# Latent attention: spreading transfers of full height, mean squares and denominators in one slot and one PSUM bank, division before the last additions

## The reference, cut to what matters

```
xn = layernorm(x, ln_x_g, ln_x_b)
ln = layernorm(latents, ln_l_g, ln_l_b)
q = (ln @ Wq).reshape(b, m, h, d).transpose(0, 2, 1, 3)
kv = jnp.concatenate([xn @ Wkv, ln @ Wkv], axis=1)
qn = rmsnorm(q, qn_g) * scale
kn = rmsnorm(k, kn_g)
sim = jnp.einsum('bhid,bhjd->bhij', qn, kn)
attn = jax.nn.softmax(sim.astype(jnp.float32), axis=-1).astype(sim.dtype)
out = jnp.einsum('bhij,bhjd->bhid', attn, v)
return out @ Wout + bout
```

## Time and profile before

| | |
|---|---|
| median of 3 runs | 1456.08 us |
| profiled execution, its own time | 1462.04 us |
| its span | 1460.3 us |
| TensorE busy (matmuls) | 1300.3 us, 89% |
| VectorE, ACT, GpSimd busy | 811.0, 637.5, 558.7 us |
| granted TensorE clock, mean of the span | 0.949 |
| spreading transfers of roots, of denominators | 232 and 124, 64.0 KB each |

### The profile page before, as it was taken

One profiled execution on the slowest core, in us unless ns is written; L12 is line 12 of the kernel. 1 busy time (PEld: TensorE's weight loads), 2 busy tenths in 40 slices (PEclk: granted clock), 3 DMA queues, 4 the chain that ended last, 5 costly groups with the idle time before them and its releaser, 6 DMA issues. The chain is left out here.

```text
span 1460.3 us, 20536 instructions
## 1 busy us (share of the span) xinstructions
PE 1300.3 (89%) x7179; PEld 561.9 (38%) x7179; DVE 811.0 (56%) x1364; ACT 637.5 (44%) x1187; POOL 558.7 (38%) x517
## 2 busy tenths in 40 slices
PE   5879789759997899999999999999967998887998
PEld 2214332238972333333333333333234774223443
DVE  4767677363336566655665666566455444623654
ACT  4454535442225555545553555454332444453222
POOL 1012201057421646554665555556605770310000
PEclk9999899779999999999999999999977999797999
DMA  9500400249622022222222222222051124000530
GB/s 267 215 1 12 117 6 1 100 170 370 245 104 65 12 45 46 44 44 41 47 44 44 44 44 45 43 45 44 22 188 35 52 52 127 1 1 0 118 72 15
DMA packets 68593, 109.14 MB, mean 75 GB/s; under 512 B 13278, under 2 KB 51550, under 8 KB 67742
## 3 DMA queue, kind: packets, MB, share of 16 engines
q1 hardware_dynamic: 56524, 93.80, 24.0%
q0 software_dynamic: 4544, 9.32, 2.3%
q10 hardware_dynamic: 7424, 4.72, 1.1%
HBM read 76.56 MB, written 11.04 MB: 60 GB/s over the span
## 5 line engine op out<-in xcount | busy, mean ns | idle before, releaser
L2693 ACT ACTIVATE a_prob<-a_TP 128x512 f32<-128x512 f32 x256 | 139.0, 595 | 161.6 <-PE a_TP L2448 161.6
L2844 DVE TENSOR_REDUCE a_lat<-a_SP 128x2 f32<-128x1024 f32 x128 | 156.1, 1220 | 85.0 <-PE a_SP L2412 85.0
L2980 POOL TENSOR_TENSOR a_acc<-a_prob 128x512 f32<-128x512 f32 x64 | 80.0, 1270 | 219.4 <-PE a_MS L2472 216.9
L2444 PE MATMUL a_TP<-a_qn,a_kn 64*128 64x512 f32 x512 | 146.7, 641 | 1.5 <-ACT a_prob L2693 1.5
L2460 PE MATMUL a_MS<-a_prob,a_V 128*64 128x512 f32 x512 | 129.5, 605 | 0.2 <-ACT a_prob L2693 0.2
L3543 DVE TENSOR_REDUCE a_nm<-a_A 128x8 bf16<-128x616 f32 x84 | 66.8, 795 | 39.2 <-PE a_A L3226 39.2
L2984 POOL TENSOR_TENSOR a_acc<-a_acc,a_prob 77x512 f32<-77x512 f32 x64 | 79.8, 1268 | 0.0
L2989 POOL TENSOR_TENSOR a_acc<-a_acc,a_prob 128x512 f32<-128x512 f32 x64 | 79.8, 1268 | 0.0
L2866 DVE TENSOR_TENSOR a_acc<-a_acc,a_prob 128x512 f32<-128x512 f32 x64 | 75.6, 1221 | 6.4 <-ACT a_prob L2693 6.3
L3757 POOL TENSOR_TENSOR a_on<-a_osb,a_rden 128x512 f32<-128x512 f32 x9 | 11.5, 1281 | 163.8 <-ACT a_osb L3426 163.8
L2444 PEld LDWEIGHTS a_TP<-a_qn,a_kn 64*128 64x128 f32 x512 | 39.7, 184 | 80.0 <-issue 51.3
(11 more groups left out here) (565 smaller groups left out, 2738.2 us busy)
## 6 DMA issues: line engine op xcount, KB each, us to landing
ring_w<-in_F_w SPq DMA_DIRECT2D x64, 512.0 KB, 12.3
a_rn<-a_rms_rows SPq DMA_DIRECT2D x232, 64.0 KB, 2.4
a_rden<-a_den_rows SPq DMA_DIRECT2D x124, 64.0 KB, 2.1
f_wide<-weight_rows SPq DMA_DIRECT2D x24, 256.0 KB, 5.5
a_maskT<-in_maskT SPq DMA_DIRECT2D x1, 2304.0 KB
a_biasT<-in_biasT SPq DMA_DIRECT2D x1, 2304.0 KB
f_b<-in_F_b SPq DMA_DIRECT2D x1, 2048.0 KB, 7.9
token_rows<-f_xtok ACTq DMA_DIRECT2D x8, 256.0 KB, 5.8
```

Of the source, the lines that this page charges most:

```text
L2444: nc.tensor.matmul(TP[0:n, h, :], keys(h), qn[half(h), r % 4, :], start=True, stop=False)
L2693: nc.scalar.activation(prob[0:n, 2 * k + h, :], TP[0:n, h, :], ACT.Exp, bias=rowneg[0:n, b:b + 1] if k == 0 else 0.0).then_inc(p_ready, 1)
L2844: nc.vector.tensor_reduce(lat[:, g % 2, 2 * u:2 * u + 2], SP[:, :, :], AX.X, ALU.max, negate=True).then_inc(s_used, 1)
L2980: nc.gpsimd.tensor_tensor(acc[:, h, :], prob[:, 2 + h, :], prob[:, 4 + h, :], ALU.add).then_inc(added, 1)
```

## The change

It has four parts.
- **Transfers.** Each root transfer now takes 32 source rows and writes all 128 partitions of `rn` (two for q, two for k, where there were four and four); each denominator transfer takes 64 rows and writes all 128 partitions of `rden` (two for four). The denominators' tiles change places for that. SP's order in a round is q, k, denominators as before in rounds up to 7, and q, denominators, k from round 8 on. A round issues six transfers of 128 KB where it issued twelve of 64 KB.
- **Statistics.** The denominators go to columns 256 to 511 of the bank, the mean squares stay in 0 to 255. `means(r + 3)` moves from step 1 to step 2, directly ahead of `sums(r - 1)`; `values(r - 1, 4)` moves from step 2 to step 1. TensorE no longer waits for the clip between them. Instead VectorE's clip waits for the denominators' matmuls (`den_made`), and ACT's logarithm of the denominators for the clip (`ms_clipped`).
- **Order behind it.** On VectorE `keep_output` stands ahead of reduction 3 and the clip behind it. On ACT `rms` moves behind the third exponentials, directly ahead of `denominators`.
- **Division.** On GpSimd `divide(r - 1)` moves ahead of the third pair of additions.

```diff
--- before.py
+++ after.py
@@ -2270,28 +2270,33 @@
                 sp.dma_start(blk[:, :], d["blk64"]).then_inc(blk_in, 16)
                 sp.dma_start(Wv[:, :], d["A2_Wv"]).then_inc(v_in, 16)
                 sp.dma_start(Wo[:, :, :], d["A2_Wo"]).then_inc(o_in, 16)
+                def spread_roots(g, j, normed, spread):
+                    sp.wait_ge(ms_rms, g + 1)
+                    sp.wait_ge(normed, g)
+                    for n in range(2):
+                        at = 32 * (2 * j + n)
+                        sp.dma_start(rn[:, j, n * HS:(n + 1) * HS],
+                                     rms_rows[at:at + 32, :].rearrange("i (c t) -> i c t", c=1)
+                                     .broadcast_to([32, 4, HS])).then_inc(spread, 16)
+
+                def spread_denominators(r):
+                    sp.wait_ge(den_ready, r + 1)
+                    if r:
+                        sp.wait_ge(o_normed, r)
+                    for n in range(2):
+                        sp.dma_start(rden[:, n * HS:(n + 1) * HS],
+                                     den_rows[HD * n:HD * n + HD, :].rearrange("i (c t) -> i c t", c=1)
+                                     .broadcast_to([HD, 2, HS])).then_inc(den_spread, 16)
+
                 for r in range(R):
-                    g = r + RAW
-                    if g < R:
-                        sp.wait_ge(ms_rms, g + 1)
-                        for j, normed, spread in ((0, q_normed, q_spread), (1, k_normed, k_spread)):
-                            sp.wait_ge(normed, g)
-                            for n in range(2):
-                                for h in range(2):
-                                    at = 32 * (2 * j + n) + 16 * h
-                                    sp.dma_start(rn[half(h), j, n * HS:(n + 1) * HS],
-                                                 rms_rows[at:at + 16, :].rearrange("i (c t) -> i c t", c=1)
-                                                 .broadcast_to([16, 4, HS])).then_inc(spread, 16)
-                    if r:
-                        sp.wait_ge(den_ready, r)
-                        if r >= 2:
-                            sp.wait_ge(o_normed, r - 1)
-                        for h in range(2):
-                            for n in range(2):
-                                at = 32 * (2 * h + n)
-                                sp.dma_start(rden[half(h), n * HS:(n + 1) * HS],
-                                             den_rows[at:at + 32, :].rearrange("i (c t) -> i c t", c=1)
-                                             .broadcast_to([32, 2, HS])).then_inc(den_spread, 16)
+                    if r + RAW < R:
+                        spread_roots(r + RAW, 0, q_normed, q_spread)
+                    if r >= 2 * B:
+                        spread_denominators(r - 1)
+                    if r + RAW < R:
+                        spread_roots(r + RAW, 1, k_normed, k_spread)
+                    if 0 < r < 2 * B:
+                        spread_denominators(r - 1)
 
             @block.tensor
             def _(pe):
@@ -2468,8 +2473,8 @@
                             mm = nc.tensor.matmul(DEN[half(h), :], ones64[:, :], acc[:, h, :], start=True, stop=True)
                             continue
                         for n in range(2):
-                            at = 32 * (2 * h + n)
-                            mm = nc.tensor.matmul(DEN[at:at + 32, 0:HS], ones64[:, 0:32],
+                            at = 32 * (2 * n + h)
+                            mm = nc.tensor.matmul(DEN[at:at + 32, HS:S], ones64[:, 0:32],
                                                   acc[:, h, n * HS:(n + 1) * HS], start=True, stop=True)
                     mm.then_inc(den_made, 1)
 
@@ -2553,16 +2558,14 @@
                             project(r + 3)
                         if s == 1 and r:
                             values(r - 1, 3)
-                        if s == (1 if r else 2):
+                            values(r - 1, 4)
+                        if s == 2:
                             if r == 0:
                                 pe.wait_ge(n_shifted, B + 1)
                             if r + 3 < R:
                                 means(r + 3)
-                        if s == 2 and r:
-                            values(r - 1, 4)
-                            if r + 3 < R:
-                                pe.wait_ge(ms_clipped, r + 4)
-                            sums(r - 1)
+                            if r:
+                                sums(r - 1)
                         if s == 3:
                             if p == 0 and b:
                                 output(b - 1, O, range(NP))
@@ -2700,11 +2703,13 @@
 
                 def denominators(r):
                     act.wait_ge(den_made, r + 1)
+                    if r + 4 < R:
+                        act.wait_ge(ms_clipped, r + 5)
                     if r < R - 1:
-                        nc.scalar.activation(lnd[:, 0:HS], DEN[:, 0:HS], ACT.Ln).then_inc(den_log, 1)
+                        nc.scalar.activation(lnd[:, 0:HS], DEN[:, HS:S], ACT.Ln).then_inc(den_log, 1)
                         act.wait_ge(den_log, r + 1)
                         if r:
-                            act.wait_ge(den_spread, 64 * r)
+                            act.wait_ge(den_spread, 32 * r)
                         nc.scalar.activation(den_rows[:, :], lnd[:, 0:HS], ACT.Exp, scale=-1.0).then_inc(den_ready, 1)
                         return
                     nc.scalar.activation(lnd[:, :], DEN[:, :], ACT.Ln).then_inc(den_log, 1)
@@ -2754,7 +2759,7 @@
                         if k == (0 if r else 1) and r + 3 < R:
                             square_q(r + 3)
                             square_k(r + 3)
-                        if k == (1 if r else 3) and r + 3 < R:
+                        if k == (2 if r else 3) and r + 3 < R:
                             rms(r + 3)
                         if k == 2 and r:
                             denominators(r - 1)
@@ -2766,6 +2771,8 @@
                     dve.wait_ge(ms_ready, g + 1)
                     if g:
                         dve.wait_ge(ms_log, g)
+                    if g > RAW:
+                        dve.wait_ge(den_made, g - RAW)
                     if g >= RAW:
                         nc.vector.tensor_scalar(clip[:, 0, 0:HS], MS[:, 0, 0:HS], 1.0 / HD, 1e-16, ALU.mult,
                                                 ALU.max).then_inc(ms_clipped, 1)
@@ -2775,7 +2782,7 @@
 
                 def norm_q(g):
                     if g >= RAW:
-                        dve.wait_ge(q_spread, 64 * (g - RAW + 1))
+                        dve.wait_ge(q_spread, 32 * (g - RAW + 1))
                     else:
                         dve.wait_ge(ms_rms, g + 1)
                     nc.vector.scalar_tensor_tensor(out=qn[:, g % 4, :], in0=QP[:, :], scalar=cv[:, 0:1],
@@ -2783,7 +2790,7 @@
 
                 def norm_k(g):
                     if g >= RAW:
-                        dve.wait_ge(k_spread, 64 * (g - RAW + 1))
+                        dve.wait_ge(k_spread, 32 * (g - RAW + 1))
                     else:
                         dve.wait_ge(ms_rms, g + 1)
                     nc.vector.scalar_tensor_tensor(out=kn[:, g % 4, :], in0=KP[:, :], scalar=vec[:, 5:6],
@@ -2932,14 +2939,12 @@
                         normal(4)
                     if r + 1 < R:
                         reduce(r + 1, 2)
-                    if 0 < r < R - 3:
-                        clip_means(r + 3)
+                    if r:
+                        keep_output(r - 1)
                     if r + 1 < R:
                         reduce(r + 1, 3)
-                    if r == 0:
+                    if r + 3 < R:
                         clip_means(r + 3)
-                    if r:
-                        keep_output(r - 1)
                     if r + 1 < R:
                         reduce(r + 1, 4)
                         combine(r + 1)
@@ -2972,6 +2977,12 @@
                     pool.wait_ge(c_normed, i + 1)
                     nc.gpsimd.tensor_copy(kncb[:, 2 * i:2 * i + 2, :], knc[:, 2 * i:2 * i + 2, :]).then_inc(c_cast, 1)
 
+                def divide(r):
+                    pool.wait_ge(o_kept, r + 1)
+                    pool.wait_ge(den_spread, 32 * (r + 1))
+                    nc.gpsimd.tensor_tensor(on[:, r % NP, :], on[:, r % NP, :], rden[:, :],
+                                            ALU.mult).then_inc(o_normed, 1)
+
                 def add_chunks(r):
                     for h in range(2):
                         pool.wait_ge(p_ready, r * 2 * NK + 5 + h)
@@ -2983,6 +2994,8 @@
                         pool.wait_ge(added, r * 6 + h + 1)
                         nc.gpsimd.tensor_tensor(acc[0:SK, h, :], acc[0:SK, h, :], prob[0:SK, h, :],
                                                 ALU.add).then_inc(added, 1)
+                    if r:
+                        divide(r - 1)
                     for h in range(2):
```

(8 more changed lines are left out.)

## The result

The change makes the kernel slower: 1495.95 us, the median of four runs (1489.29 to 1500.93), beside 1456.5 us for the kernel before on the same chip. The ratio is 1.0262, with a 95% interval of 1.0232 to 1.0292. That is +39.5 us where +18.2 were forecast. The profiled execution took 1498.66 us for a span of 1496.9 us. Medians here are over all runs of a kernel; the ratios leave out the few runs that were 1.7 to 5% longer at a lower clock.

What follows compares the result with a forecast made beforehand. The prediction took TensorE to bound the kernel, with one chain only 0.4 us from late. Terms +21.8, +1.1, -4.2 and -0.5 sum to +18.2 us, giving a median of 1474.3 us, range 1456 to 1497.

Steps and rivals of the forecast that it cites:

- the chain: Mean squares, clip, root, spreading transfers, normalised k, negated maximum, next round's scores matmul on TensorE; 0.4 us of slack claimed.
- the rival of the paced engines: DMA engines paced by the roots' price: 0.88 us a transfer, sixth lands 1.25 us later, 1497 us; chance 0.12.
- So these rounds last 17.70 us: Rounds 9 to 15, 17 to 23, 25 to 28: 17.70 us each where TensorE alone would need 16.3; +21.8 us in all.
- rounds 2 to 7 at +1.1 us: GpSimd's division ahead of its last additions keeps a round from going under some 17.55 us: +0.2 x 6.
- the output rounds at -4.2: Rounds 8, 16 and 24: the output projection's 1.21 us wait for the division goes, 3 x (-1.2 - 0.2).
- The landing kept at 2.44 us: From issue of the last k root transfer to the start of k's normalisation, kept at 2.44 us despite 128 partitions.
- The clip's new wait for the denominators' matmuls: On VectorE, claimed covered: 1.2 us until those matmuls are seen, against 1.25 us of the reduction.
- the term put at nothing on ACT: Denominators' logarithm and exponential delay the fourth exponentials by about 1 us; no cost taken for TensorE's last scores.
- rivals of cheap issues: SP issues a full-height transfer every 0.48 us: 1457 us, or 1451 with 2.1 us landing; together chance 0.18.
- issue time by rows: Each full-height transfer takes 1.26 us to issue on SP, 3.15 us more a round: 1550 us; chance 0.04.
- the 2.1 that the prediction set beside it: New root transfers landing like the denominators', in 2.1 us: round 17.36 us, the sum 6.1 us less.
- The loop through the division: Rounds 2 to 7: denominators landed at 16.0, division 1.6, last additions, reduction, second maxima; round not under some 17.55 us.

Runs made afterwards that it cites:

- 1447.14: Kernel before with only the six full-height spreading transfers (order q, k, denominators) and VectorE's last additions behind the next round's first reduction: 1447.14 us, ratio 0.9913.
- 1442.65: Kernel before with six full-height transfers always in order q, k, denominators, division ahead, last additions late, statistics in their old place: 1442.65 us, ratio 0.9895.
- 1582.06: Kernel before with full-height transfers and late last additions, but k's roots in eight pieces of 32 partitions and q's in four: 1582.06 us, ratio 1.0835.
- eight-piece kernel: Kernel before with full-height transfers and late last additions, but only k's roots in eight pieces of 32 partitions, q's in two transfers: 1506.37 us, ratio 1.0313.

## Why the prediction was right and where it was wrong

The forecast had the sign, the chain and the range (1456 to 1497, which holds 1495.95 at its very end, where the rival of the paced engines had put it), and less than half of the size. **The step that failed most is "So these rounds last 17.70 us"**: it gave a wait no price beyond its own length, and in the runs drops of the granted clock came with seven of the waits. Two more terms were wrong: rounds 2 to 7 at +1.1 us, which measured +7.3, and the output rounds at -4.2, which measured +1.2. The landing kept at 2.44 us was too small, with less effect.

In the profiled executions the attention grew by 43.3 us for the forecast's 18.2. Of these 25.1 us some 14 are the clock's, 6.2 are in rounds 2 to 7, 3.7 in the output rounds and 2.3 in the 18 late rounds besides the clock; the rest is under 1 us.

**The matmuls and the clip: right.** Mean squares at 7.25 us forecast, 7.32 measured; clip 8.50 and 8.57; first issue 9.85 and 9.90. The clip's new wait for the denominators' matmuls cost nothing, and neither did the term put at nothing on ACT: all of TensorE's waits for exponentials in L2449 and L2465 come to 1.5 us in the whole span.

**Issues: right.** A full-height transfer is issued every 0.60 to 0.62 us, with 0.70 between pairs; from the first to the sixth 3.15 forecast, 3.2 measured in most late rounds (3.48 in round 14, whose second q transfer took longer, 0.86). The rivals of cheap issues and of issue time by rows are both refuted, the second by the 0.72 us of a quarter-height piece as well.

**Landing: mis-sized.** "I keep 2.44" became 2.7; the 2.1 that the prediction set beside it was further off still. With 0.3 us of landing and 0.07 each at the mean squares and in the queue a quiet late round is 18.13 us and not 17.70. The DMA share of the late rounds is 0.20, and was 0.28, so the engines paced nothing, and the rival that gave 1497 was right only in its number. That the measured time lies inside the range is luck in the same sense: the range's upper end stood for that rival.

**The count of rounds: wrong.** I took 18 rounds at 17.70. Rounds 9, 17 and 25 follow the long output rounds, don't wait, and take 16.25. In return rounds 16 and 24 begin with the same wait. If no clock had dropped, these 18 rounds would be 14 at 18.13, one at 17.39 (round 28) and three at 16.25, 320.0 us or +21.6: the errors of landing and count cancel to the forecast's +21.8, by luck. The measured stretch is +32.6. Five of its rounds had a lowered clock, at 1.7 us each 8.5 us; the remaining 2.5 us are longer waits, like the 2.02 us of round 11 beside 1.69.

**The clock: missed.** "So these rounds last 17.70 us" took for granted that a wait costs its own length. Where TensorE is busy throughout, a wait of 1.8 to 2.9 us can be followed by a stretch at 1.2 GHz. In the attention this is seven drops: some 8.5 us in the 18 rounds, 1.7 in round 16, and up to 3.4 of the +3.9 us of round 29, whose drop is twice as long. That makes some 14 us, over half of the 25.1. That waits have to do with the drops is seen in both directions: none in the late rounds of the two kernels that don't wait (1447.14 and 1442.65), in nearly every waiting round of the one that waits longest (1582.06). The length of a wait alone doesn't decide it, though. The eight-piece kernel waited 1.5 to 1.8 us in its late rounds at full clock. In the changed kernel the clock fell after 1.76 us in round 19 and not around the 2.03 us of round 24; and round 20 waits 1.98 us both there, with a drop, and in the kernel with the division put back, without one.

**Rounds 2 to 7: the mechanism right, the price wrong.** The loop through the division was there, and decided: putting the division back returned 7.1 of the 7.3 us. The forecast was +1.1, by a floor of 17.55 us (its own terms give 17.4: 16.0 + 1.6 + 2.49 + 0.64 + 1.21 - 4.55), and a round measured 18.54. Nearly half of what is missing is the tail behind the landing. The forecast took "the last addition on VectorE (0.64, half of the 1.28 of a pair)", behind both of GpSimd's additions. Measured, VectorE's pair starts behind the first of them and takes 2.68 us beside the second and the casts, as in round 4 of the changed kernel:

```profile
567.56 1.26 POOL L3002 TENSOR_TENSOR a_acc<-a_acc,a_prob 128x512 f32<-128x512 f32 x1
567.70 2.68 DVE L2873 TENSOR_TENSOR a_acc<-a_acc,a_prob 128x512 f32<-128x512 f32 x2 [1.41 <-POOL a_acc L3002]
...
568.77 1.07 POOL L2970 CAST a_qnb<-a_qn 128x512 bf16<-128x512 f32 x1
...
571.58 0.39 PE L2417 MATMUL a_SP<-a_knb,a_qnb 64*128 64x512 bf16 x2 [0.97 <-DVE a_lat L2851]
```

From the start of the division (565.11) to these maxima it is 6.47 us, and the forecast's terms make 5.94. The row for the 1.28 us came from round 8, with nothing beside it; the price was to be taken from a round in which GpSimd works, and the earlier trace rows show GpSimd adding right up to that place. As much again is the way from the denominators' last issue to the division, 2.58 us where the forecast had 2.1.

**Output rounds: the wait went, the gain didn't come.** -4.2 us forecast, +1.2 measured. The wait for the division is gone, as said, and where nothing else is late it brings 1.34 us a round (24.92 to 23.58). But rounds 16 and 24 pay the wait at their start, round 16 a drop of the clock as well, and round 8 pays 1.2 us to the last additions (24.50, and 23.34 with them late).

**Rounds 0, 1 and 30:** -1.7 us; the forecast had -0.5 for these and round 29 together. All parts: +32.6 + 7.3 + 1.2 + 3.9 (round 29) - 1.7 = +43.3 us.

What stays open: why the clock falls after one wait and not after another of the same length. No run here varied a wait by itself. The kernels with more and smaller transfers also change the DMA traffic, and no run separates that.
